# Maxima and turned blocks in one ring of four banks, value products in four blocks, maxima and scores over 64 rows each

## The chip, the core and the metric

The kernel runs on one core of one Trainium2 chip. The metric is the device time of one launch in microseconds. Engines are named as in the profile: PE (TensorE, matmuls; PEld is its weight loads), DVE (VectorE), ACT (ScalarE), POOL (GpSimd) and SP (SyncE, which here only issues DMAs).

## What is computed

The input x is 16 sequences of 512 tokens with 512 features. Four blocks are added to it in turn, each on a layer-normed x: a gated delta rule (the first layer), an FFN with LoRA experts, the attention that the change touches, and the same FFN again. The attention, cut to what matters:

```python
qh = q.reshape(b, s, N_QUERY, N_HEAD, D_HEAD)      # 4 x 8 heads of 16
kh = k.reshape(b, s, N_HEAD, D_HEAD)               # 8 heads of k and v
scores = jnp.einsum('bsqhd,bthd->bqhst', qh, kh) * scale
probs = jax.nn.softmax(scores, axis=-1)
a_dot = jnp.einsum('bqhst,bthd->bsqhd', probs, vh)
...
a_mem = sigma_q @ memory / (sigma_q @ memory_norm)
out = a_dot * (1.0 - w) + a_mem * w
```

## The kernel before

The first layer (up to about 2100 us) is a program of its own, `delta_rule_layer`, and no part of the change. The rest is `token_layers`: for each of 16 batches (b) an `attention(b, following)` and a `between(b, following)`. `between` holds the two FFNs and the projections of the next attention; part of the next batch's first FFN already runs at the end of `attention`. Every engine has its own hand-written order of the same steps, and semaphores join them.

PSUM is one tensor `ps` (`row_psum`) of eight banks of 128 x 512 fp32. In the attention banks 0 to 2 hold scores (STACK_BANKS = 3), banks 3 to 5 maxima (MAX_BANKS = 3), bank 6 the sums over the values, and bank 7 everything that is turned; the memory products use 6 and 7.

A head has 16 features; to keep fp32 accuracy in fp32r matmuls, q and k are stacked in parts: `q_stack` holds per pair of heads 64 rows for the even and 64 for the odd head, and `k_stack` holds for each head of k the same 128 rows with the other head's 64 rows zeroed. One row of the 64 takes the negative maximum, so that the score comes out already shifted.

`attention` runs in rounds g = 0 to 44. Round g does:

- `maximum(g, st)` for the four token tiles st of head g: a matmul 128x512 (L1618) into a bank, from which DVE takes the row maximum (L1900, `smax`). It waits for `max_ready` of the reduce three tiles back.
- `score(h, tt)` for the four tiles of head h = g - 7 (SCORE_LAG): the matmul with q and k swapped (L1631) into a bank 0 to 2; ACT writes exp into `probs` (L1361), which has 7 slots for heads. It waits for `exp_ready` three tiles back.
- in every fourth round the maxima of four heads (a "quad") are turned (L1673, four transposes of `smax`), ACT copies them negated into `shift` (L1368), and four small DMAs on SP write them into `q_stack`, for which the scores of these heads wait (`shift_in`).
- `values(quad, half)`: the probabilities of four heads times `v_aug` (L1642), 128x32 tiles side by side, eight matmuls in each of two blocks per quad, in rounds with (i, j) in AV_SLOTS = ((1, 1), (3, 0)); j is the half of the round. ACT copies the sum (L1377, `av_sb`), PE turns it (L1691), DVE divides by the sums of exp (L1890, L1894, `av_n`), and POOL adds it to x (L1243).
- in rounds 5 to 8 `memory(t)`: matmuls with `mem_aug` (L1605), and DVE's L1875 to L1880.

Each head's exp may overwrite a slot of `probs` when the values of the head seven before are done:

```python
if h >= PROBS and tt == 0:
    act.wait_ge(av_mm, at(b, 2 * QUADS, 2 * ((h - PROBS) // 4 + 1)))
```

The order within half a round on PE is: maximum, score, [transposes of the maxima], [a value block], maximum, score. In the picks of k (L1577, L1578: `pick_k`) the matmuls take 32 rows each, at different rows of the array.

## Time and profile before

| | us |
|---|---|
| median of 3 runs | 5277.39 |
| lowest, highest | 5273.88, 5286.0 |
| the profiled execution's own time | 5281.24 |
| its span, first to last instruction | 5279.4 |
| mean granted TensorE clock | 0.965 |
| PE busy (share of the span) | 4795.7 (91%) |
| DVE busy | 3613.9 (68%) |
| ACT busy | 2392.5 (45%) |

Busy is the union of an engine's instructions. Matmuls are pipelined, so two that start 0.23 us apart are each shown with some 0.4 us, and a PE that is busy all the time may still wait; the spacing of starts tells more. The trace names tiles by their partitions: `probs` in a row can also be the memory's or the norm's scratch, which share its room. The attention of one batch that the rows below come from (batch 4) runs from 2969.9 to 3106.0 us of the span.

### The profile page before, as it was taken

To read this page: it belongs to the slowest core of one execution; us is meant where nothing else is said; L and a number is where in the kernel's file an instruction comes from. 1 tells how busy PE (TensorE), PEld (TensorE's weight loads), DVE (VectorE), ACT (ScalarE), POOL (GpSimd) and SP (SyncE) were. 2 spreads that over 40 slices of the span, in tenths; PEclk is the share of its full clock that TensorE was granted. 3 is DMA by queue.
4 is the path that set the end of the run, shared out by engine and by line. 5 is a ranking of instruction groups with operands and counts; after the bars stand their busy time and mean duration, and the time that the engine had idled before them with its cause. 6 is when DMAs were issued, how large, how long until landed. Compare 5 with 4: busy or idle time off the path is not lost.

```text
span 5279.4 us, 144356 instructions
## 1 busy us (share of the span) xinstructions
PE 4795.7 (91%) x63104; PEld 3487.2 (66%) x63104; DVE 3613.9 (68%) x7890; ACT 2392.5 (45%) x4592; POOL 714.3 (14%) x909
## 2 busy tenths in 40 slices
PE   4799999999999995799999999999999999999998
PEld 4678877777787774565665665665665665666564
DVE  3667776666677673667767767767766766766765
ACT  2234333333333342346446446445545545545544
POOL 0000000000000000121121121121122121121121
PEclk9899999989999997899999999999999999999999
DMA  2223222222222222000000000000000000000000
GB/s 59 52 63 75 60 60 64 64 62 65 70 59 60 67 68 59 27 1 17 17 9 9 17 17 1 17 17 1 17 17 1 17 17 1 17 17 1 17 9 9
DMA packets 352132, 171.74 MB, mean 33 GB/s; under 512 B 300016, under 2 KB 300784, under 8 KB 350736
## 3 DMA queue, kind: packets, MB, share of 16 engines
q1 hardware_dynamic: 342528, 145.20, 10.4%
q10 hardware_dynamic: 8976, 17.30, 1.2%
q8 instruction: 499, 8.18, 0.7%
q14 instruction: 129, 1.06, 0.1%
HBM read 93.74 MB, written 67.63 MB: 31 GB/s over the span
## 4 chain that ended last, share of the span: by engine, by line
PE 45%; DVE 10%; ACT 3%; issue 1%; DMA 1%; POOL 1%; SPq 0%; DVEq 0%; ACTq 0%; POOLq 0%
PE row_psum L1642 9%; PE row_psum L1631 8%; PE row_psum L1618 8%; DVE smax L1900 5%; PE row_psum L40 5%; PE row_psum L42 5%; PE row_psum L41 5%; PE row_psum L1673 1%; ACT xr_hi L1287 1%; PE row_psum L1691 1%; ACT probs L1361 1%; DVE probs L1880 1%; PE row_psum L1426 1%; PE row_psum L1605 1%; PE row_psum L1586 0%
## 5 line engine op out<-in xcount | busy, mean ns | idle before, releaser
L1900 DVE TENSOR_REDUCE smax<-row_psum 128x1 f32<-128x512 f32 x2048 | 1261.9, 683 | 271.0 <-PE row_psum L1618 270.3
L1361 ACT ACTIVATE probs<-row_psum 128x512 f32<-128x512 f32 x2048 | 1080.8, 607 | 592.9 <-PE row_psum L1631 370.6
L1618 PE MATMUL row_psum<-k_stack,q_stack 128*128 128x512 f32 x2048 | 864.8, 431 | 33.3 <-DVE smax L1900 24.4
L1631 PE MATMUL row_psum<-q_stack,k_stack 128*128 128x512 f32 x2048 | 849.0, 426 | 25.1 <-ACT probs L1361 19.6
L1618 PEld LDWEIGHTS row_psum<-k_stack,q_stack 128*128 128x128 f32 x2048 | 389.6, 191 | 359.4 <-DVE smax L1900 231.7
L1631 PEld LDWEIGHTS row_psum<-q_stack,k_stack 128*128 128x128 f32 x2048 | 385.9, 191 | 267.3 <-ACT probs L1361 161.7
L1642 PE MATMUL row_psum<-probs,v_aug 128*32 128x512 f32 x4096 | 489.2, 598 | 0.0
L868 DVE TENSOR_TENSOR lane_t<-lane_t,lane_p 128x30 f32<-128x30 f32 (+14 forms) x960 | 318.4, 332 | 32.9
L865 DVE TENSOR_TENSOR lane_p<-lane_t 128x30 f32<-128x30 f32 (+14 forms) x960 | 316.2, 329 | 23.5
L40 PE MATMUL span_bank<-x_hi,w_hi 128*128 128x256 f32 x1024 | 304.8, 298 | 30.2 <-DVE x_lo L841 30.1
L40 PE MATMUL row_psum<-wf_hi,xr_hi 128*128 128x320 f32 (+1 forms) x1024 | 327.4, 320 | 0.5 <-DVE xr_lo L1768 0.3
L42 PE MATMUL row_psum<-wf_hi,xr_lo 128*128 128x320 f32 (+1 forms) x1024 | 319.8, 312 | 0.0
L41 PE MATMUL row_psum<-wf_lo,xr_hi 128*128 128x320 f32 (+1 forms) x1024 | 318.8, 311 | 0.0
L41 PE MATMUL span_bank<-x_lo,w_hi 128*128 128x256 f32 x1024 | 291.9, 285 | 0.6 <-issue 0.6
L42 PE MATMUL span_bank<-x_hi,w_lo 128*128 128x256 f32 x1024 | 292.0, 285 | 0.0
L1243 POOL TENSOR_TENSOR xs<-xs,av_n 128x256 f32<-128x256 f32 x128 | 93.4, 729 | 1452.3 <-DVE av_n L1894 1452.3
L263 POOL TENSOR_TENSOR o_lo<-og_both,o_hi 128x512 fp32r<-128x512 f32 x64 | 93.1, 1474 | 1328.2 <-DVE tri L883 1242.1
L1642 PEld LDWEIGHTS row_psum<-probs,v_aug 128*32 128x32 f32 x4096 | 108.4, 109 | 220.7 <-issue 185.8
L366 ACT ACTIVATE og_both<-og_both 128x512 f32<-128x512 f32 x64 | 40.3, 630 | 468.1 <-DVE og_both L918 468.1
L40 PEld LDWEIGHTS span_bank<-x_hi,w_hi 128*128 128x128 f32 x1024 | 199.0, 194 | 42.8 <-ACT x_hi L299 34.7
L1890 DVE RECIPROCAL av_rc<-row_psum 128x16 f32<-128x16 f32 x128 | 32.2, 252 | 277.7 <-PE row_psum L1691 277.7
L1327 ACT ACTIVATE q_stack<-row_psum 128x512 fp32r<-128x512 f32 x256 | 154.1, 609 | 148.8 <-PE row_psum L1586 145.3
(209 smaller groups left out, 9816.1 us busy)
## 6 DMA issues: line engine op xcount, KB each, us to landing
x_sp<-in_x ACTq DMA_DIRECT2D x33, 512.0 KB, 4.0
tri_dram<-tri SPq DMA_DIRECT2D x256, 64.0 KB, 2.0
lane_t<-tri_dram SPq DMA_DIRECT2D x32, 512.0 KB, 4.8
inv_dram<-lane_t SPq DMA_DIRECT2D x32, 512.0 KB, 2.6
inv_b<-inv_dram SPq DMA_DIRECT2D x256, 64.0 KB, 2.3
x_res<-in_x SPq DMA_DIRECT2D x32, 512.0 KB, 3.8
x<-x_res SPq DMA_DIRECT2D x32, 512.0 KB, 3.8
xs<-x SPq DMA_DIRECT2D x16, 1024.0 KB, 5.5
```

The lines of the kernel that those rows point to most:

```text
L40: pe.matmul(out, a_hi, b_hi, start=first, stop=False)
L41: pe.matmul(out, a_hi, b_lo, start=False, stop=False)
L42: return pe.matmul(out, a_lo, b_hi, start=False, stop=last)
L865: mark(dve.tensor_tensor(prod, lane_t[:, 0:m, m:m + 1].to_broadcast([P, m, n]), lane_t[:, m:m + 1, m + 1:NB].to_broadcast([P, m, n]), ALU. ...
L868: mark(dve.tensor_tensor(lane_t[:, 0:m, m + 1:NB], lane_t[:, 0:m, m + 1:NB], prod, ALU.add))
L1243: pool.tensor_tensor(xq, xq, av_n[:, :, :, :].rearrange("p t h e -> p t (h e)"), ALU.add).then_inc(adot_added, 1)
L1327: act.activation(q_stack[:, m, :], ps[:, (HP + m) % STACK_BANKS, :], ACT.Copy).then_inc(qstack_ready, 1)
L1361: act.activation(probs[:, h % PROBS, tt, :], ps[:, m % STACK_BANKS, :], ACT.Exp, scale=float(DH) ** -0.5).then_inc(exp_ready, 1)
L1618: pe.matmul(ps[:, STACK_BANKS + m % MAX_BANKS, :], q_stack[:, qt, P * st:P * st + P], k_stack[:, kv, :], start=True, stop=True).then_inc(m ...
L1631: pe.matmul(ps[:, m % STACK_BANKS, :], k_stack[:, kv, P * tt:P * tt + P], q_stack[:, qt, :], start=True, stop=True).then_inc(score_mm, 1)
L1642: last = pe.matmul(ps[32 * e:32 * e + 32, 6, :], v_aug[:, tt, h % NKV, :], probs[:, h % PROBS, tt, :], start=tt == 0, stop=tt == NT - 1)
L1900: dve.tensor_reduce(smax[:, g, st:st + 1], ps[:, STACK_BANKS + (NT * g + st) % MAX_BANKS, :], AX.X, ALU.max).then_inc(max_ready, 1)
```

## The change

Three things change, all in `attention`.

First, the maxima's banks, the transposes of the maxima (maxT) and the turned values (avT) share one ring. `ring_of_banks` walks through the rounds when the program is built and gives each user the bank that was given out longest ago; before round 9 the ring is banks 3, 4, 5, from round 9 bank 7 joins it (it belonged to the memory products until then). The last quad's maxT and the avT from round 31 on keep bank 7. Each user waits for whoever was in its bank before (`ring_bank`), and for nothing else.

Second, `values` has four blocks per quad, one per tile tt, at the start of four rounds in a row (j == 0). The order of accumulation is the same. `exp` waits tile by tile for them where the head is the last of a quad.

Third, while maxima and scores run in the same round (maxima in rounds 7 to 31, scores of heads 0 to 24), their matmuls read only the 64 rows of their own head (`rows_of`): maximum g the rows of kv = g % 8, score g - 7 those of the other half. The rows left out are the zeroed ones of `k_stack`.

```diff
 SCORE_LAG = 7
 AV_LAG = SCORE_LAG + 1
-AV_SLOTS = ((1, 1), (3, 0))
...
-MAX_BANKS = 3
+RING = (3, 4, 5)
+RING_LAST = 7
...
+        def ring_of_banks():
+
+            order, place, inside = list(RING), {}, {RING_LAST: ("memory", NT - 1)}
+
+            def put(kind, n, bank=None):
+                bank = order[0] if bank is None else bank
+                order.remove(bank)
+                order.append(bank)
+                place[kind, n] = bank, inside[bank] if bank in inside else None
+                inside[bank] = kind, n
+
+            for g in range(NH + OUT_LAG):
+                if g == MEM_LAG + NT:
+                    order.insert(0, RING_LAST)
+                for st in range(NT):
+                    if g < NH:
+                        put("max", NT * g + st)
+                    quad, i = divmod(g - MAXT_LAG, 4)
+                    if (i, st) == (0, 2) and 0 <= quad < QUADS:
+                        put("maxT", quad, RING_LAST if quad == QUADS - 1 else None)
+                quad, i = divmod(g - 3 - TURN_LAG, 4)
+                if i == 0 and 0 <= quad < QUADS:
+                    put("avT", quad, RING_LAST if 4 * quad + 3 + TURN_LAG >= NH - 1 else None)
+            return place
...
+                                if h >= PROBS and h % 4 == PROBS % 4 and tt:
+                                    act.wait_ge(av_mm, at(b, NT * QUADS, NT * ((h - PROBS) // 4) + tt + 1))
                                 if h >= PROBS and tt == 0:
-                                    act.wait_ge(av_mm, at(b, 2 * QUADS, 2 * ((h - PROBS) // 4 + 1)))
+                                    act.wait_ge(av_mm, at(b, NT * QUADS, NT * ((h - PROBS) // 4) + (1 if h % 4 == PROBS % 4 else NT)))
...
+            def rows_of(kv, paired):
+
+                return slice(64 * (kv % 2), 64 * (kv % 2) + 64) if paired else slice(0, P)
+
             def attention(b, following):
 
                 def memory(t):
...
-                        pe.wait_ge(shift_ready, at(b, QUADS, 1))
...
+                def ring_bank(kind, n):
+
+                    bank, inside = in_ring[kind, n]
+                    if inside is not None:
+                        of, k = inside
+                        if of == "max":
+                            pe.wait_ge(max_ready, at(b, NT * NH, k + 1))
+                        elif of == "maxT":
+                            pe.wait_ge(shift_ready, at(b, QUADS, k + 1))
+                        elif of == "avT":
+                            pe.wait_ge(avn_ready, at(b, QUADS, k + 1))
+                        else:
+                            pe.wait_ge(amem_ready, at(b, NT, k + 1))
+                    return bank
+
                 def maximum(g, st):
...
-                    elif m >= MAX_BANKS:
-                        pe.wait_ge(max_ready, at(b, NT * NH, m - MAX_BANKS + 1))
-                    pe.matmul(ps[:, STACK_BANKS + m % MAX_BANKS, :], q_stack[:, qt, P * st:P * st + P], k_stack[:, kv, :],
+                    bank = ring_bank("max", m)
+                    rows = rows_of(kv, g >= SCORE_LAG)
+                    pe.matmul(ps[:, bank, :], q_stack[rows, qt, P * st:P * st + P], k_stack[rows, kv, :],
                               start=True, stop=True).then_inc(max_mm, 1)
...
-                    pe.matmul(ps[:, m % STACK_BANKS, :], k_stack[:, kv, P * tt:P * tt + P], q_stack[:, qt, :],
+                    rows = rows_of(kv, h + SCORE_LAG < NH)
+                    pe.matmul(ps[:, m % STACK_BANKS, :], k_stack[rows, kv, P * tt:P * tt + P], q_stack[rows, qt, :],
                               start=True, stop=True).then_inc(score_mm, 1)
 
-                def values(quad, half):
-
-                    pe.wait_ge(exp_ready, at(b, NT * NH, NT * (4 * quad + 3) + 2 * half + 2))
-                    if half == 0 and quad:
+                def values(quad, tt):
+
+                    pe.wait_ge(exp_ready, at(b, NT * NH, NT * (4 * quad + 3) + tt + 1))
+                    if tt == 0 and quad:
                         pe.wait_ge(av_ready, at(b, QUADS, quad))
...
                             pe.wait_ge(max_ready, at(b, NT * NH, 16 * quad + 16))
-                            if quad:
-                                pe.wait_ge(shift_ready, at(b, QUADS, quad))
-                            if quad == 1:
-                                pe.wait_ge(amem_ready, at(b, NT, NT))
-                            if turned_before(quad):
-                                pe.wait_ge(avn_ready, at(b, QUADS, turned_before(quad)))
+                            bank = ring_bank("maxT", quad)
...
                         quad, i = divmod(g - 3 - AV_LAG, 4)
-                        if (i, j) in AV_SLOTS and 0 <= quad < QUADS:
-                            values(quad, AV_SLOTS.index((i, j)))
+                        if j == 0 and 0 <= quad < QUADS:
+                            values(quad, i)
```

The order on PE in a round with transposes of the maxima (round 28), from its first maximum on, before (L1618 maximum, L1631 score, L1673 those transposes, L1642 a value block):

```order
L1618 MATMUL row_psum<-k_stack,q_stack 128x512 [waits max_ready,qstack_ready]
L1631 MATMUL row_psum<-q_stack,k_stack 128x512 [waits exp_ready]
L1618 MATMUL row_psum<-k_stack,q_stack 128x512 [waits max_ready]
L1631 MATMUL row_psum<-q_stack,k_stack 128x512 [waits exp_ready]
L1618 MATMUL row_psum<-k_stack,q_stack 128x512 [waits max_ready]
L1631 MATMUL row_psum<-q_stack,k_stack 128x512 [waits exp_ready]
L1673 MATMUL row_psum<-ident,smax 4x128 [waits avn_ready,shift_ready,max_ready]
L1673 MATMUL row_psum<-ident,smax 4x128 x3
L1642 MATMUL row_psum<-probs,v_aug 32x512 [waits av_ready,exp_ready]
L1642 MATMUL row_psum<-probs,v_aug 32x512 x7
L1618 MATMUL row_psum<-k_stack,q_stack 128x512 [waits max_ready]
L1631 MATMUL row_psum<-q_stack,k_stack 128x512 [waits exp_ready]
```

And in the same round now (L1661 maximum, L1675 score, L1713 transposes, L1687 a value block):

```order
L1661 MATMUL row_psum<-k_stack,q_stack 128x512 [waits max_ready,qstack_ready]
L1675 MATMUL row_psum<-q_stack,k_stack 128x512 [waits exp_ready]
L1687 MATMUL row_psum<-probs,v_aug 32x512 [waits exp_ready]
L1687 MATMUL row_psum<-probs,v_aug 32x512 x3
L1661 MATMUL row_psum<-k_stack,q_stack 128x512 [waits max_ready]
L1675 MATMUL row_psum<-q_stack,k_stack 128x512 [waits exp_ready]
L1661 MATMUL row_psum<-k_stack,q_stack 128x512 [waits max_ready]
L1675 MATMUL row_psum<-q_stack,k_stack 128x512 [waits exp_ready]
L1713 MATMUL row_psum<-ident,smax 4x128 [waits avn_ready,max_ready]
L1713 MATMUL row_psum<-ident,smax 4x128 x3
L1661 MATMUL row_psum<-k_stack,q_stack 128x512 [waits max_ready]
L1675 MATMUL row_psum<-q_stack,k_stack 128x512 [waits exp_ready]
```

The eight value matmuls behind the transposes have become four behind the round's first score (the other four of that eight now come one round earlier, in the same place); the transposes no longer wait for `shift_ready`, and a maximum of the next round does instead.

The order on ACT before, from the first round in which the values are summed (L1361 exp, L1377 the copy av_sb):

```order
L1361 ACTIVATE probs<-row_psum 128x512 [waits score_mm] x4
L1361 ACTIVATE probs<-row_psum 128x512 [waits av_mm,score_mm]
L1361 ACTIVATE probs<-row_psum 128x512 [waits score_mm]
L1377 ACTIVATE av_sb<-row_psum 128x512 [waits av_mm]
L1361 ACTIVATE probs<-row_psum 128x512 [waits score_mm] x2
L1361 ACTIVATE probs<-row_psum 128x512 [waits av_mm,score_mm]
L1361 ACTIVATE probs<-row_psum 128x512 [waits score_mm] x3
L1361 ACTIVATE probs<-row_psum 128x512 [waits av_mm,score_mm]
L1361 ACTIVATE probs<-row_psum 128x512 [waits score_mm] x3
```

And now (L1386 exp, L1402 av_sb):

```order
L1386 ACTIVATE probs<-row_psum 128x512 [waits score_mm] x4
L1386 ACTIVATE probs<-row_psum 128x512 [waits av_mm,score_mm] x2
L1402 ACTIVATE av_sb<-row_psum 128x512 [waits av_mm]
L1386 ACTIVATE probs<-row_psum 128x512 [waits av_mm,score_mm] x3
L1386 ACTIVATE probs<-row_psum 128x512 [waits score_mm] x3
L1386 ACTIVATE probs<-row_psum 128x512 [waits av_mm,score_mm]
```

The instructions stand in the same order; where four exps of the last head of a quad waited once for all of the value products, each now waits for its own tile's.

## Rows read from the trace of the kernel before

**Rows 1.** The page's first line.
```profile
span 5279.4 us, 144356 instructions
```

**Rows 2.** Windows: one batch's stages; start:end, length, busy time of each engine (instructions), clock.
```profile
2969.90:2995.70 25.80, 22.79 (x100) 14.96 (x101) 24.24 (x49) 14.22 (x26) 4.26 (x4) 1.00 0.01 4
2995.70:3008.30 12.60, 10.60 (x43) 7.30 (x41) 11.11 (x22) 8.22 (x16) 2.10 (x2) 0.86 0.01 1
3008.30:3071.20 62.90, 62.83 (x349) 34.04 (x347) 48.68 (x85) 43.19 (x86) 2.90 (x4) 1.00 0.01 2
3071.20:3106.00 34.80, 32.23 (x202) 17.34 (x202) 15.66 (x37) 19.18 (x41) 10.90 (x15) 1.00 0.01 2
3106.00:3164.40 58.40, 54.20 (x324) 47.63 (x322) 40.55 (x97) 17.17 (x41) 16.89 (x24) 1.00 0.11 36
```

**Rows 3.** Waits in 3008.28 to 3071.22: who waited for whom; us, times, longest.
```profile
DVE smax L1900 <- PE row_psum L1618: 14.1, 10, 1.8
...
ACT probs L1361 <- PE row_psum L1642: 7.9, 5, 1.6
```

**Rows 4.** The chain that ended last, 3000 to 3075: start us, us, what.
```profile
3022.22 0.47 PE row_psum L1673 x4
...
3061.49 0.47 PE row_psum L1673 x4
```

**Rows 5.** Timeline of PE, 3021.2 to 3026.6: start us, us, instruction, count.
```profile
3021.59 0.39 PE L1618 MATMUL row_psum<-k_stack,q_stack 128*128 128x512 f32 x1
3021.82 0.40 PE L1631 MATMUL row_psum<-q_stack,k_stack 128*128 128x512 f32 x1
3022.09 0.60 PE L1673 MATMUL row_psum<-ident,smax 128*4 128x128 f32 x4
3022.62 1.92 PE L1642 MATMUL row_psum<-probs,v_aug 128*32 128x512 f32 x16
3024.47 0.50 PE L1618 MATMUL row_psum<-k_stack,q_stack 128*128 128x512 f32 x1
```

**Rows 6.** Timeline of DVE, 3013 to 3030; brackets: idle before, and its releaser.
```profile
3017.04 4.28 DVE L1900 TENSOR_REDUCE smax<-row_psum 128x1 f32<-128x512 f32 x7 [1.45 <-PE row_psum L1618]
3021.24 0.25 DVE L1890 RECIPROCAL av_rc<-row_psum 128x16 f32<-128x16 f32 x1
...
3021.86 1.88 DVE L1900 TENSOR_REDUCE smax<-row_psum 128x1 f32<-128x512 f32 x3
```

**Rows 7.** Timeline of ACT, 3013 to 3030.
```profile
3012.64 0.57 ACT L1368 ACTIVATE shift<-row_psum 4x512 fp32r<-4x512 f32 x1
3013.12 2.00 ACT L1361 ACTIVATE probs<-row_psum 128x512 f32<-128x512 f32 x4
```

**Rows 8.** Timeline of PE, 2962.2 to 2964.0: picks of k between products of q.
```profile
2962.66 0.39 PE L42 MATMUL row_psum<-xr_hi,wq_lo 128*128 128x512 f32 x1
2962.97 0.51 PE L1577 MATMUL row_psum<-xat_hi,sel 32*128 32x512 f32 x3
2963.31 0.40 PE L1578 MATMUL row_psum<-xat_lo,sel 32*128 32x512 f32 x3
2963.64 0.50 PE L40 MATMUL row_psum<-xr_hi,wq_hi 128*128 128x512 f32 x1
```

**Rows 9.** Waits in the tail, 3071.2 to 3106.
```profile
PEld row_psum L1631 <- ACT probs L1361: 6.4, 13, 0.8
ACT probs L1361 <- PE row_psum L1642: 6.1, 2, 3.1
```

**Rows 10.** Windows in the first layer, at a fall of the clock.
```profile
1493.20:1498.10 4.90, 4.90 (x129) 4.76 (x128) 4.90 (x10) 2.89 (x6) 0.00 (x0) 1.00 0.65 102
1498.40:1501.80 3.40, 3.40 (x9) 2.64 (x9) 2.92 (x4) 0.00 (x0) 2.27 (x2) 0.50 0.50 76
```

**Rows 11.** Timeline of PE, 1493 to 1503.
```profile
1493.17 5.04 PE L551 MATMUL span_bank<-kq 32*64 32x128 f32 x128
```

**Rows 12.** Timeline of SP's queue, 3012 to 3017.
```profile
3013.24 2.39 SPq L1199 DMA_DIRECT2D q_stack<-shift  x4
```

More of the change, by code:

```diff
@@ L1150, in head, with bank_of @@
             return divmod(4 * quad + i, NKV)
-        def turned_before(quad):
-            return sum(4 * q + 3 + TURN_LAG < 4 * quad + MAXT_LAG for q in range(QUADS))
-        def maxima_before(quad):
-            return sum(4 * q + MAXT_LAG <= 4 * quad + 3 + TURN_LAG for q in range(QUADS))
+        def ring_of_banks():
[19 more added lines that the diff above has]
+            return place
+        in_ring = ring_of_banks()
+        def bank_of(kind, n):
+            return in_ring[kind, n][0]
         def in_order(begin, attention, between):
@@ L1686, in attention @@
                         pe.wait_ge(av_ready, at(b, QUADS, quad + 1))
[L1687 to L1689 removed]
+                        bank = ring_bank("avT", quad)
                         for t in range(NT):
[L1691 removed]
+                            last = pe.transpose(ps[:, bank, P * t:P * t + P], av_sb[:, P * t:P * t + P], ident2[:, :])
                         last.then_inc(avT_mm, 1)
```

29 lines of the change are left out of this document (13 added, 16 removed).

## The prediction

> **What bounds the kernel now.** I read the span first [rows 1], then cut one batch into stages [rows 2]. Batches repeat every 194.5 us, and 16 of them fill the second layer. The five stages are: rounds 0 to 7 (25.8 us), rounds 8 to 11 (12.6 us), rounds 12 to 31 up to the first reduce of round 31 (62.9 us), the tail with the last scores (34.8 us), and the work between two attentions (58.4 us). The reader is to see that the third stage is the longest, that PE is busy in all of it, and that DVE (48.68 of 62.90) and ACT (43.19) are not. "Busy" for PE includes the flight of pipelined matmuls, so the spacing of starts is what counts below.
>
> The chain through that stage passes the transposes of the maxima at regular places, 3022.22 and 3061.49, three periods of four rounds apart [rows 4]: 13.1 us for four rounds. The sum of PE's work in four rounds comes from the spacing of starts [rows 5]. A maximum or a score starts 0.23 us after its predecessor (3021.59, 3021.82), so 32 of them take 7.5 us. A block of value products (16 instructions in the trace, since each of the 8 matmuls is fp32 and runs as two) holds PE for 1.85 us (3022.62 to 3024.47), two blocks 3.7 us. The two groups of four transposes take about 0.5 us each (3022.09 to 3022.62). Together 12.2 us of 13.1; the other 0.9 us are waits. PE is the bound.
>
> DVE comes next. Seven reduces follow each other in 4.2 us, 0.60 us each, and the normalising of four heads takes 0.62 us (3021.24 to 3021.86) [rows 6]. Four rounds need 16 x 0.60 + 0.62 = 10.2 us. The wait table says where the rest goes: DVE waited 14.1 us in this stage for L1618, in ten waits of up to 1.8 us [rows 3], that is, it ran dry in each 1.85 us block. ACT's four exps take 2.00 us including the last one's 0.57, so 0.48 us apart, and a shift copy costs it 0.48 us (3012.64 to 3013.12) [rows 7]. With av_sb priced like the shift, four rounds need 16 x 0.48 + 2 x 0.48 = 8.6 us. ACT also stood 7.9 us before an exp that must not overwrite probabilities until both value blocks are done [rows 3].
>
> **The change, part by part.**
>
> *64 rows in opposite halves.* Heads g and g-7 have kv of opposite parity, so in rounds 7 to 31 the maximum reads one half of the array's rows and the score the other. Does PE run them side by side? The trace has the same kind of matmul: the three picks of k at L1577 are fp32r, 128 columns wide, 512 long, on different 32-row groups and into different banks, and all three stand in one piece of 0.51 us, with the next three beginning 0.34 us after (2962.97, 2963.31) [rows 8]. Three full-height matmuls would need 0.7 us. So I take them as parallel: a pair costs 0.235 us in place of 0.47, 16 pairs 3.8 us instead of 7.5. The lower bound is this; the upper bound is 0.47 (no overlap).
>
> *Changes of tile shape.* The step from full height to 32-row tiles took 0.31 us instead of 0.23 (2962.66 to 2962.97), and back 0.33 us (2963.31 to 2963.64) [rows 8]: 0.1 us per change. The Trainium skill ("TensorEngine Tiling (Array Packing)", Tiling Modes, Key Properties) says that changing the tiling mode drains the engine, which speaks against a change that multiplies such places; by this trace the drain costs about 0.1 us.
>
> *Four value blocks of 4 matmuls.* The matmuls are the same, so a block holds PE for half of 1.85, 0.93 us, plus a change of shape on each side: 1.13 us, four of them 4.5 us instead of 3.7. With the transposes at 1.2 us (their changes included) PE's sum for four rounds is 3.8 + 4.5 + 1.2 = 9.5 us. That is below DVE's 10.2 us. What queues behind a block is a pause of about 1.4 us for DVE (score, block, next maximum), and four banks hold 2.4 us of reduces, where three banks (1.8 us) did not cover 1.85 us plus a score.
>
> *The ring.* The turns no longer own bank 7: a transpose takes the oldest of four banks. What it waits for is a reduce that the next maximum would have waited for anyway, and a maximum that follows in its bank waits for ACT's shift copy (round 4q+5, third tile), about 2 us after the transposes; it is hidden behind three other banks. Transposes of the maxima waited for the normalising of the last turn, and in round 8 for the last memory reduction; the second wait goes. Until round 9 there are only three banks, so rounds 0 to 7 keep their 25.8 us (DVE is busy 24.24 of them [rows 2]).
>
> *ACT's finer waits.* The exp of every fourth head now waits tile by tile; the 7.9 us of waits shrink, but ACT isn't the bound, so they are worth nothing in this stage by themselves.
>
> *The shift through SP.* Four small DMAs take 2.39 us from the first issue [rows 12]. From the transposes to the first score that needs them lie 2.5 rounds, 6.7 us at the new pace. Transposes 0.5, wait for ACT and copy about 1.8, DMAs 2.4: 4.7 us. Covered by 2 us; if the cover went, each 1 us would cost 8 x 16 = 128 us at most.
>
> **The sum.** DVE becomes the bound. The new period lies between 10.2 us (no waits left) and 10.2 + 0.9 (as much waiting as now); blocks are half as long, so I take two thirds of 0.9: 10.8 us. The third stage has 19 rounds, 4.75 periods: 4.75 x (13.1 - 10.8) = 10.9 us. In rounds 8 to 11 DVE is idle 1.5 us (12.60 less 11.11), mostly at the wait that goes: 1.0 us. In the tail ACT stood 6.1 us for value blocks and PE's loads 6.4 us for ACT [rows 9], but the 34.8 us hold much other PE work and the changes of shape grow by 0.6 us; between 0 and 3 us, I take 1.2. Nothing for the last stage. Per batch 13.1 us, for 16 batches 210 us. The profiled execution took 5281.2 us (span 5279.4), the median is 5277.4: 5281.2 - 210 = 5071, against the median 5067. I forecast **5067 us**. With no waits left (14.1 + 1.5 + 1.2 = 16.8 us, 269 us) it is 5008; with 0.9 us of waits and nothing in the tail, 9.5 + 1.0 = 10.5 us, 5109.
>
> **Rivals.**
>
> *Weights of the same half can't be loaded under its running matmul.* Then each half needs load and stream in turn. The first matmuls after a change show this spacing, 0.34 us (2962.97 to 2963.31) [rows 8], for a pair: 16 x 0.34 = 5.4 us, PE's sum 11.1 us, period 11.7, saving 4.75 x 1.4 + 1.5 = 8.2 us per batch, **5147 us**. For it speaks that the trace never has a long run of such pairs; against it, that at full height the next load runs under the current matmul, which the 0.23 us spacing shows [rows 5]. The Trainium skill ("TensorE: Matmul & The Clock Gate", Part 3, The mechanism) says that a weight load overlaps matmuls in flight only when the row group differs or it goes to the background buffer; by its first half the time would be this one. The 0.23 us at full height speaks for the second half.
>
> *The clock.* PE will be less dense. After five microseconds of nothing but 32-row tiles (L551) the granted clock fell from 1.00 to 0.50, that is from 2.4 to 1.2 GHz, for 3.4 us [rows 10, 11], and in rounds 8 to 11, where PE waited, the mean is 0.86 [rows 2]. If 64-row matmuls count for less than full ones and a quarter of the third stage runs at 1.2 GHz, PE's sum is 1.25 x 9.5 = 11.9, period 12.5, saving 2.9 + 1.5 = 4.4 us, **5207 us**. Against it: pairs fill all 128 rows together, the value blocks are full height, and the sum says PE streams some nine tenths of the period. A fall in rounds 8 to 10 alone costs nothing, since a pair at 1.2 GHz (0.47 us) is still shorter than a reduce.
>
> *Slower: the pairs don't overlap.* They are 128 columns wide and each waits on its own semaphore; if the second is held until the first has left the array, PE's sum is 7.5 + 4.5 + 1.2 = 13.2 us, with 0.6 us of waits 13.8: 0.7 us more per period, 3.3 us per batch, less about 1 us of waits saved in rounds 8 to 11: 2.3 x 16 = 37 us, **5314 us**. It decides from a pair spacing of (13.1 - 0.6 - 5.7) / 16 = 0.43 us on. Against it stands L1577.
>
> **How the numbers follow.** DVE-bound as forecast 0.62 (own range 5008 to 5109); same-half loading 0.14; clock 0.09; no overlap 0.09, of which 0.07 end slower and 0.02 the same; something in between that gives back nearly all 0.06 (0.03 faster, 0.03 same). A measurement of this kernel tells some 0.2%, 10 us, from no change. So faster 0.88, same 0.05, slower 0.07. The range takes in the first two cases: 5008 to 5150.
>
> **What would show it.** Right: the period of four rounds falls from 13.1 to 10.4 to 11.1 us; DVE's idle before the reduce in the third stage falls from 14.1 to under 4 us and the chain there passes through the reduces; score and maximum of a pair start within 0.05 us of each other while pairs follow at 0.24 us when nothing waits; the value blocks stand at 0.9 to 1.0 us; rounds 0 to 7 and the last stage keep 25.8 and 58.4 us. Wrong: a pair spacing of 0.34 or 0.47 us in a run of pairs; a granted clock well under 1.00 in the third stage; score waiting for the shift DMAs; or waits moved to ACT, whose three banks are unchanged: if ACT becomes the partner that runs dry, the waits exceed 0.9 us.

## The result, and the profile after

The changed kernel takes **5091.56 us** (median of 4 runs, 5087.94 to 5102.96) against 5280.30 us of the kernel before in the same session (4 runs): ratio 0.9645, 95% interval 0.9628 to 0.9662. Forecast were 5067 us and 5008 to 5150.

The page's first line, and its groups of the reduce and the exp (busy us, mean ns, idle before). On the page of before DVE stood 271.0 us ahead of its reduces.

```profile
span 5091.6 us, 144724 instructions
...
L1938 DVE TENSOR_REDUCE smax<-row_psum 128x1 f32<-128x512 f32 x2048 | 1269.3, 681 | 90.9 <-PE row_psum L1661 90.4
L1386 ACT ACTIVATE probs<-row_psum 128x512 f32<-128x512 f32 x2048 | 1096.6, 602 | 378.1 <-PE row_psum L1675 358.5
```

The windows of one batch's five stages (batch 4), as in [rows 2]: length, busy time of PE, PEld, DVE, ACT, POOL, granted clock.

```profile
2921.90:2948.00 26.10, 22.49 (x99) 14.34 (x100) 24.39 (x48) 14.16 (x26) 4.21 (x4) 1.00 0.01 3
2948.00:2958.80 10.80, 9.76 (x57) 4.77 (x55) 10.73 (x21) 8.15 (x16) 2.17 (x2) 1.00 0.01 2
2958.80:3011.90 53.10, 51.97 (x344) 21.09 (x340) 49.08 (x85) 43.85 (x86) 2.94 (x4) 1.00 0.01 2
3011.90:3045.80 33.90, 30.71 (x201) 16.34 (x194) 15.76 (x37) 19.70 (x40) 10.63 (x15) 1.00 0.01 2
3045.80:3104.20 58.40, 54.24 (x324) 47.63 (x321) 40.41 (x97) 17.08 (x41) 16.90 (x24) 1.00 0.11 37
```

Set against [rows 2], the third stage fell from 62.9 to 53.1 us and the second from 12.6 to 10.8, where the clock is now 1.00 instead of 0.86. The other three moved by less than a microsecond here. DVE is busy 49.08 of 53.10 us in the third stage; it was 48.68 of 62.90. PE still reads 51.97, because a matmul in flight counts as busy; that number doesn't tell whether PE is the bound. The last stage keeps its 58.40.

The waits of that stage, 2958.8 to 3011.9 (compare [rows 3]):

```profile
PEld row_psum L1661 <- DVE smax L1938: 15.9, 19, 0.8
ACT probs L1386 <- PE row_psum L1675: 8.1, 14, 0.8
DVE smax L1938 <- PE row_psum L1661: 3.9, 14, 0.8
PEld row_psum L1675 <- DMA q_stack<-shift: 3.1, 5, 1.1
```

DVE's wait for the maxima fell from 14.1 to 3.9 us, and no wait for value products is among the large ones. What rose is PE's: its weight loads wait 15.9 us for a reduce, where they waited 8.9 before. In [rows 3] DVE mostly waited for PE, now PE waits for DVE. That wait alone proves little, since run e1 below, which PE bounds, has 12.6 us of it; what speaks for DVE as the pace is that it is busy in 92% of the stage (49.08 of 53.10). One sign that the prediction named did not come: the chain of work that ended last doesn't pass through the reduces. In the two traces they are 3.2% of it around this stage now and were 5.1% before; the rest is mostly PE, whose matmuls in flight leave the chain hardly a gap through which to step to another engine.

PE's timeline from 2970.4 (compare [rows 5]; start, us, instruction):

```profile
2970.43 0.39 PE L1661 MATMUL row_psum<-k_stack,q_stack 64*128 64x512 f32 x1
2970.43 0.39 PE L1675 MATMUL row_psum<-q_stack,k_stack 64*128 64x512 f32 x1
...
2971.94 1.06 PE L1687 MATMUL row_psum<-probs,v_aug 128*32 128x512 f32 x8
2972.93 0.49 PE L1661 MATMUL row_psum<-k_stack,q_stack 64*128 64x512 f32 x1
...
2973.27 0.39 PE L1661 MATMUL row_psum<-k_stack,q_stack 64*128 64x512 f32 x1
...
2973.51 0.39 PE L1661 MATMUL row_psum<-k_stack,q_stack 64*128 64x512 f32 x1
```

Maximum and score of a pair start in the same 10 ns, pairs follow at 0.23 to 0.24 us, and a value block of 8 instructions holds PE from 2971.94 to 2972.93, 0.99 us. The first pair after it needs 0.34 us (2972.93 to 2973.27), so the change of shape costs the expected 0.1 us there.

DVE's timeline over one period (compare [rows 6]; in brackets idle time and its releaser):

```profile
2969.52 0.25 DVE L1928 RECIPROCAL av_rc<-row_psum 128x16 f32<-128x16 f32 x1
...
2970.14 3.07 DVE L1938 TENSOR_REDUCE smax<-row_psum 128x1 f32<-128x512 f32 x5
2973.47 2.48 DVE L1938 TENSOR_REDUCE smax<-row_psum 128x1 f32<-128x512 f32 x4 [0.26 <-PE row_psum L1661]
2976.10 2.48 DVE L1938 TENSOR_REDUCE smax<-row_psum 128x1 f32<-128x512 f32 x4 [0.15 <-PE row_psum L1661]
2978.89 1.89 DVE L1938 TENSOR_REDUCE smax<-row_psum 128x1 f32<-128x512 f32 x3 [0.31 <-PE row_psum L1661]
2980.70 0.25 DVE L1928 RECIPROCAL av_rc<-row_psum 128x16 f32<-128x16 f32 x1
```

From reciprocal to reciprocal lie 11.18 us, where 13.1 lay before. Three pauses remain, 0.26 + 0.15 + 0.31 = 0.72 us, each behind a value block.

### The profile page after: what moved, and what is told of

Its sections match the earlier page's. It is cut to its first block, busy times and chain, and to the rows that moved or that the text cites. A ratio compares the mean times of both kernels' runs of the same rounds, so it can differ in the third digit from the quotient of the medians.

```text
span 5091.6 us, 144724 instructions
## 1 busy us (share of the span) xinstructions
PE 4591.6 (90%) x63104; PEld 3229.5 (63%) x63104; DVE 3620.3 (71%) x7890; ACT 2409.6 (47%) x4592; POOL 716.3 (14%) x909
## 3 DMA queue, kind: packets, MB, share of 16 engines
q1 hardware_dynamic: 342528, 145.20, 10.7%
## 4 chain that ended last, share of the span: by engine, by line
PE 43%; DVE 10%; ACT 3%; issue 1%; POOL 1%; DMA 1%; SPq 0%; DVEq 0%; ACTq 0%; POOLq 0%
PE row_psum L1687 9%; PE row_psum L1661 9%; PE row_psum L40 5%; DVE smax L1938 5%; PE row_psum L42 5%; PE row_psum L41 5%; PE row_psum L1675 4%; PE row_psum L1729 1%; ACT xr_hi L1310 1%; PE row_psum L1713 1%; DVE probs L1918 1%; PE row_psum L1451 1%; DVE stats L1772 1%; POOL rstd L1253 1%; PE row_psum L1633 1%
## 5 line engine op out<-in xcount | busy, mean ns | idle before, releaser
L1386 ACT ACTIVATE probs<-row_psum 128x512 f32<-128x512 f32 x2048 | 1096.6, 602 | 378.1 <-PE row_psum L1675 358.5
L1661 PE MATMUL row_psum<-k_stack,q_stack 64*128 64x512 f32 (+1 forms) x2048 | 738.3, 437 | 50.6 <-DVE smax L1938 24.4
L1675 PE MATMUL row_psum<-q_stack,k_stack 64*128 64x512 f32 (+1 forms) x2048 | 761.6, 447 | 17.4 <-DMA q_stack<-shift 4.4
L1661 PEld LDWEIGHTS row_psum<-k_stack,q_stack 64*128 64x128 f32 (+1 forms) x2048 | 350.5, 186 | 504.1 <-DVE smax L1938 374.0
L1687 PE MATMUL row_psum<-probs,v_aug 128*32 128x512 f32 x4096 | 539.5, 604 | 2.3 <-ACT av_sb L1402 0.8
L1675 PEld LDWEIGHTS row_psum<-q_stack,k_stack 64*128 64x128 f32 (+1 forms) x2048 | 340.9, 185 | 211.7 <-ACT probs L1386 152.3
L1315 ACT ACTIVATE probs<-row_psum 128x64 f32<-128x64 f32 x256 | 52.3, 229 | 331.4 <-PE row_psum L42 331.4
```

Source lines behind the costliest of these rows:

```text
L1386: act.activation(probs[:, h % PROBS, tt, :], ps[:, m % STACK_BANKS, :], ACT.Exp, scale=float(DH) ** -0.5).then_inc(exp_ready, 1)
L1661: pe.matmul(ps[:, bank, :], q_stack[rows, qt, P * st:P * st + P], k_stack[rows, kv, :], start=True, stop=True).then_inc(max_mm, 1)
L1675: pe.matmul(ps[:, m % STACK_BANKS, :], k_stack[rows, kv, P * tt:P * tt + P], q_stack[rows, qt, :], start=True, stop=True).then_inc(score_m ...
L1687: last = pe.matmul(ps[32 * e:32 * e + 32, 6, :], v_aug[:, tt, h % NKV, :], probs[:, h % PROBS, tt, :], start=tt == 0, stop=tt == NT - 1)
```

## The experiments

Stages below are medians over the 16 batches, in us, worked out from each trace: rounds 0 to 7, rounds 8 to 11, rounds 12 to 31, the tail (the cuts of [rows 2]; the time between attentions is 58.4 in all of them). "rows" is 64 rows each, "ring" the ring of four banks, "blocks" the four value blocks. The kernel before took 5278.5, 5276.7 and 5283.9 us beside the three groups of experiments (e1 to e4, e5 to e8, e9 to e12); each ratio is taken within its group. Every kernel but the one before and e2 also lets each exp wait for its own tile's values only; no run has that alone.

| | rows, ring, blocks | median us | ratio, 95% | 0-7 | 8-11 | 12-31 | tail |
|---|---|---|---|---|---|---|---|
| before | none | 5277.4 | 1 | 25.85 | 12.70 | 62.96 | 34.62 |
| after | all | 5091.6 | 0.9645 (0.9628-0.9662) | 26.16 | 10.79 | 52.70 | 34.24 |
| e2 | rows | 5282.4 | 1.0002 (0.9982-1.0021) | 25.85 | 12.38 | 63.22 | 34.49 |
| e12 | ring | 5283.1 | 0.9999 (0.9985-1.0014) | 27.12 | 10.80 | 63.43 | 34.85 |
| e9 | blocks | 5255.2 | 0.9958 (0.9941-0.9976) | 25.83 | 12.97 | 61.93 | 33.31 |
| e3 | rows, ring | 5283.9 | 1.0006 (0.9993-1.0019) | 27.17 | 10.79 | 62.53 | 35.66 |
| e1 | ring, blocks | 5235.5 | 0.9916 (0.9887-0.9946) | 26.16 | 10.79 | 61.79 | 34.21 |
| e6 | rows, blocks | 5139.2 | 0.9734 (0.9718-0.9750) | 25.83 | 14.33 | 53.88 | 33.07 |
| e4 | all, same half | 5226.0 | 0.9899 (0.9871-0.9927) | 26.16 | 10.98 | 60.81 | 34.16 |
| e5 | e3, first block half a round earlier | 5257.6 | 0.9965 (0.9949-0.9982) | 26.16 | 10.79 | 61.12 | 36.58 |
| e7 | all, two shift DMAs | 5092.6 | 0.9644 (0.9627-0.9661) | 26.17 | 10.79 | 52.69 | 34.25 |
| e8 | all, block ahead of the score | 5237.6 | 0.9928 (0.9912-0.9943) | 26.15 | 10.79 | 59.61 | 36.38 |
| e10 | e3, half exps | 5204.9 | 0.9853 (0.9834-0.9872) | 27.11 | 10.79 | 59.46 | 35.36 |
| e11 | all, half exps | 5042.2 | 0.9539 (0.9523-0.9556) | 26.16 | 10.79 | 50.65 | 33.34 |

Medians over the batches hide the clock. In rounds 0 to 7 a batch has one of two lengths, in every kernel: where the mean granted clock of the stage was 0.94 or 0.95 instead of 1.00, it took 0.7 to 1.0 us longer. That befell 1 of 16 batches of the kernel before, 3 of the changed kernel, 1 of e1, 6 of e7, but 9 of e3, 10 of e10 and 11 of e12, and so the medians of these three read 27.1 to 27.2. In rounds 12 to 31 the clock stayed at 1.00 in the kernels without long blocks (e8 and e6 dip in one batch) and in those with long blocks and full rows (before, e12); with long blocks and 64 rows (e2, e3, e5, e10) its mean is 0.98. The batches of these four in which it stayed at 1.00 took 61.7, 61.4, 59.5 and 58.2 us.

**e1, all rows again.**

```diff
 def rows_of(kv, paired):
-    return slice(64 * (kv % 2), 64 * (kv % 2) + 64) if paired else slice(0, P)
+    return slice(0, P)
```

> The changed kernel with the ring and the four value blocks, but every maximum and score over all 128 rows. Theory (PE was the bound, and the halves running side by side relieve it): PE's sum for four rounds is 7.5 + 4.0 to 4.5 + 1.2 = 12.7 to 13.2 us, so the period stays at 12.9 to 13.8 us and the time is 5240 to 5320 us; maxima and scores start 0.23 us apart. Rival (the gain comes from the buffering: a fourth bank and shorter blocks keep DVE fed, and PE had slack): the period is 11 to 12 us and the time under 5190 us.

5235.5 us. The third stage is back at 61.8 us. Its window (length, PE, PEld, DVE, ACT, POOL, clock):

```profile
3011.20:3073.00 61.80, 61.80 (x344) 32.89 (x340) 50.05 (x86) 44.43 (x86) 2.92 (x4) 1.00 0.01 1
```

PE is busy in all 61.80 us, and this time the starts say the same: one whole period, from the value block at 3030.47 to that at 3043.53, is 13.06 us, and nothing in it waits: maxima and scores start 0.23 us apart, with 0.1 us more at each change of shape. PE's sum for this case, from the prediction's terms, is 7.5 + 4.5 + 1.2 = 13.2. With full rows and four blocks PE is the bound. By the same starts a block costs 1.00 us and 0.1 on either side. Two blocks of 1.85 us in place of four of 1.00 would make PE's sum an estimated 12.4 us, which is less than the 13.1 of the kernel before.

**e2, the rows alone**: `rows_of` in the kernel before, used by both matmuls as in the change.

> The kernel before with nothing changed but the 64 rows (three banks for the maxima, turns in bank 7, two value blocks of 8 matmuls). Theory: PE's sum falls to about 9.2 us, but a block still keeps PE away for 2.1 us or more while three banks hold 1.8 us of reduces; DVE runs dry by 0.8 to 1.0 us at each of two blocks and the period is 12.0 to 12.4 us, the time 5180 to 5220 us: about half of the gain. Rival (buffering does nothing): the time is that of the changed kernel, 5085 to 5105 us. Second rival (the 64 rows do nothing): 5270 to 5290 us.

5282.4 us, no change, and none of the three forecasts for the right reason: the time is that of the second rival, but the pairs do run side by side, and PE's sum falls by 3.7 us a period, yet the stage keeps its length. The waits of 3009.4 to 3072.7 show where it went (L1623 maximum, L1637 score, L1648 values, L1906 reduce):

```profile
DVE smax L1906 <- PE row_psum L1623: 14.5, 10, 3.2
ACT probs L1361 <- PE row_psum L1637: 12.5, 9, 3.5
ACT probs L1361 <- PE row_psum L1648: 7.9, 5, 1.6
```

DVE waits as long as in [rows 3], ten times, once per block of 1.85 us, and ACT waits 12.5 + 7.9 = 20.4 us. PE has time to spare now, but at places where nobody can use it. A part of the loss is the clock: in the five batches where it stayed at 1.00 the stage took 61.7 us, 1.3 less than before, and in the others, at 0.95 to 0.98, mostly 63.2 or more. In rounds 8 to 11 it fell to 0.60 to 0.86 in every batch. The next runs ask what holds the period at 13 us here.

**e3, the change with two blocks per quad.**

```diff
+AV_SLOTS = ((1, 1), (3, 0))
-    pe.wait_ge(exp_ready, at(b, NT * NH, NT * (4 * quad + 3) + tt + 1))
+    pe.wait_ge(exp_ready, at(b, NT * NH, NT * (4 * quad + 3) + 2 * half + 2))
-    for e in range(4):
+    for tt in (2 * half, 2 * half + 1):
+        for e in range(4):
...
-    if j == 0 and 0 <= quad < QUADS:
-        values(quad, i)
+    if (i, j) in AV_SLOTS and 0 <= quad < QUADS:
+        values(quad, AV_SLOTS.index((i, j)))
```

> The changed kernel (ring, 64 rows) with the values in two blocks of 8 matmuls at their old places. Theory: four banks hold 2.4 us, PE is away 2.0 + 0.3 + 0.3 us, so DVE runs dry by 0.2 to 0.4 us at two places in place of 0.15 to 0.35 us at four, and four changes of tile shape less: within 15 us of the changed kernel, 5080 to 5110 us. Rival (the spreading is what keeps DVE fed): 1 us more per period, 5150 us or more.

5283.9 us, the rival's side and far above the forecast: with blocks of eight, rows and ring together are worth nothing. DVE's timeline across the two blocks:

```profile
3019.25 1.88 DVE L1940 TENSOR_REDUCE smax<-row_psum 128x1 f32<-128x512 f32 x3
3022.39 3.68 DVE L1940 TENSOR_REDUCE smax<-row_psum 128x1 f32<-128x512 f32 x6 [1.26 <-PE row_psum L1662]
3027.30 4.28 DVE L1940 TENSOR_REDUCE smax<-row_psum 128x1 f32<-128x512 f32 x7 [1.23 <-PE row_psum L1662]
```

and PE's in the same stretch (L1662 maximum, L1715 transposes, L1689 values):

```profile
3019.48 0.60 PE L1715 MATMUL row_psum<-ident,smax 128*4 128x128 f32 x4 [0.21 <-DVE av_n L1934]
3020.01 1.92 PE L1689 MATMUL row_psum<-probs,v_aug 128*32 128x512 f32 x16
3021.86 0.49 PE L1662 MATMUL row_psum<-k_stack,q_stack 64*128 64x512 f32 x1
...
3023.54 0.50 PE L1662 MATMUL row_psum<-k_stack,q_stack 64*128 64x512 f32 x1 [0.72 <-ACT shift L1394]
```

DVE is dry for 1.26 and 1.23 us. The transposes wait for DVE's `av_n` (3019.48), and PE has given DVE only three maxima since; then 0.53 us of transposes, 1.85 us of block and the start of a new maximum stand against 1.88 us of reduces. The fourth bank of the ring holds the transposes here, not a maximum. After three more maxima the next one needs that bank and waits 0.72 us for ACT's shift copy, which itself is late, since ACT was dry for 2.20 us behind the same block.

**e4, both in the same half**: the maxima of rounds 7 to 31 read the half of the score.

```diff
-    rows = rows_of(kv, g >= SCORE_LAG)
+    rows = rows_of(kv + 1 if g >= SCORE_LAG else kv, g >= SCORE_LAG)
```

> The changed kernel with the maximum of rounds 7 to 31 reading the rows of the other head of its pair, so that maximum and score lie in the same half of the array (the maxima of these rounds are then not the right ones; the work is the same in size). Theory (it is the opposite halves that let two matmuls run at once, and weights load under a running matmul in the same half too): starts are 0.23 us apart, PE's sum is 12.7 to 13.2 us, the time 5240 to 5320 us, as over 128 rows. Rival (weights of the same half cannot be loaded under its running matmul): starts are 0.34 us apart, PE's sum 16 to 17 us, the time over 5500 us. Second rival (64 rows are faster by themselves): 5090 us.

5226.0 us, close to e1 (5235.5). PE's timeline (L1661 maximum, L1675 score):

```profile
2991.97 0.39 PE L1661 MATMUL row_psum<-k_stack,q_stack 64*128 64x512 f32 x1
2992.20 0.39 PE L1675 MATMUL row_psum<-q_stack,k_stack 64*128 64x512 f32 x1
2992.43 0.38 PE L1661 MATMUL row_psum<-k_stack,q_stack 64*128 64x512 f32 x1
```

Starts of one half lie 0.23 us apart, as at full height: they don't overlap, and the loads cost nothing. (Per batch 20 starts of this stage still lie within 20 ns of another, against 66 in the changed kernel, probably where the half changes from one round to the next; that would explain the 1.0 us by which e4's stage is shorter than e1's, and was not followed up.) So the gain of the rows is that they are opposite halves, not that they are fewer, and the 0.34 us spacing of [rows 8] is a cost of the change of shape, not of loading the same half. The Trainium skill ("TensorE: Matmul & The Clock Gate", Part 3, What overlaps and what doesn't) says that a weight load overlaps running matmuls only when the row group differs. This run does not agree: matmuls of one row group follow each other at 0.23 us with a load between each two.

**e5, e3 with the first block before the transposes.**

```diff
-AV_SLOTS = ((1, 1), (3, 0))
+AV_SLOTS = ((1, 0), (3, 0))
```

> As the run with two value blocks (ring, 64 rows), but the first block stands behind the round's first score instead of behind the transposes of the maxima. Theory (the block behind the transposes delayed the score, the exp and so ACT's shift copy, for which a maximum in the ring waits: 9.4 us per batch of such waits): the waits of the maximum for the shift go, the period falls from 13.0 to 11.6 to 12.1 us, the time is 5140 to 5190 us. Rival (a block of 1.85 us is simply too long for the buffers, wherever it stands): 5260 to 5290 us.

5257.6 us, the rival's side; the third stage fell by 1.4 us only, and by 1.9 in the batches at full clock (61.4 to 59.5). DVE's waits fell from 13.4 to 12.3 us, and its waits are still ten of up to 2.2 us: with the transposes out of the block's way most of the loss stays. It takes the short blocks, not another place for the long one.

**e6, no ring**: four blocks and rows, with the banks and waits of before.

```diff
-                bank = order[0] if bank is None else bank
-                order.remove(bank)
-                order.append(bank)
+                bank = RING[n % 3] if kind == "max" else RING_LAST
...
+                        pe.wait_ge(shift_ready, at(b, QUADS, 1))
```

> The changed kernel (64 rows, four value blocks) without the ring: maxima in banks 3 to 5 in turn, both kinds of transposes in bank 7 with their old waits. Theory (short blocks and the relieved PE give most, the fourth bank covers the rest): DVE holds 1.8 us while PE is away 1.0 + 0.1 + 0.3 us, so it hardly runs dry; the maxima's transposes wait for the normalising again; period 11.4 to 12.0 us, time 5100 to 5160 us. Rival (the fourth bank is decisive): period 12.5 us or more, over 5200 us.

5139.2 us, 47.6 more than with the ring. In the third stage the ring is worth only 1.2 us per batch (53.88 less 52.70), and the tail takes the same back (33.07 against 34.24). Its worth lies in rounds 8 to 11, 3.5 us per batch. Windows there, and PE's timeline (L1712 transposes, L1686 values):

```profile
2959.60:2962.70 3.10, 1.16 (x9) 0.71 (x7) 2.97 (x8) 0.60 (x1) 0.85 (x1) 1.00 0.00 0
2962.80:2966.00 3.20, 3.20 (x13) 1.60 (x13) 1.54 (x3) 1.51 (x4) 1.18 (x1) 0.52 0.00 0
...
2969.80:2971.60 1.80, 1.80 (x9) 0.20 (x8) 0.72 (x2) 0.60 (x1) 0.00 (x0) 0.50 0.00 0
```

```profile
2962.78 0.91 PE L1712 MATMUL row_psum<-ident,smax 128*4 128x128 f32 x4 [2.03 <-DVE probs L1917]
...
2969.81 1.93 PE L1686 MATMUL row_psum<-probs,v_aug 128*32 128x512 f32 x8
2971.68 0.79 PE L1660 MATMUL row_psum<-k_stack,q_stack 64*128 64x512 f32 x1
```

The transposes wait 2.03 us for the last memory product to be read out (L1917). In 2959.6 to 2962.7 PE was busy 1.16 of 3.10 us; then the granted clock is 0.52 and 0.50, that is 1.2 GHz (for 10.2 us in all, 2962.92 to 2973.16), and the value block lasts from 2969.81 to 2971.68, 1.87 us instead of 0.99. Behind it DVE was dry for 1.98 us. With the ring that wait is gone and the clock stays at 1.00 (second window of the changed kernel above).

**e7, the shift rows in two DMAs**: each writes the two rows of one parity.

```diff
-    for i in range(4):
-        n, h = head(quad, i)
-        r0 = 64 * (h % 2) + 3 * DH
-        sp.dma_start(q_stack[r0:r0 + 1, n * HP + h // 2, :], shift[i:i + 1, :]).then_inc(shift_in, 16)
+    for e in range(2):
+        r0 = 64 * e + 3 * DH
+        sp.dma_start(q_stack[r0:r0 + 1, c0:c0 + 2, :], shift[e:4:2, :]).then_inc(shift_in, 16)
```

> The changed kernel with the shift written to q_stack in two DMAs of two rows each instead of four of one row. Each issue takes about 0.6 us of the queue, so the last lands 1.2 us earlier. Theory (the scores of each fourth round wait 0.4 to 1.1 us for the DMA, and DVE runs dry by 0.3 to 0.8 us behind that): the waits for the DMA go, 0.15 to 0.45 us less per period, 5060 to 5085 us. Rival (this wait is covered by the banks, DVE being the bound): unchanged, 5085 to 5105 us.

5092.6 us, no change, because there was little to gain. The wait table above charges five idle stretches of the scores' weight loads to the DMAs, 3.1 us. But in four of the five the last DMA had landed 0.4 us before the load began, and e7 has the same stretches with nothing to release them (the changed kernel, then e7):

```profile
2976.85 0.18 PEld L1675 LDWEIGHTS row_psum<-q_stack,k_stack 64*128 64x128 f32 x1 [0.52 <-DMA q_stack<-shift]
...
2976.76 0.18 PEld L1676 LDWEIGHTS row_psum<-q_stack,k_stack 64*128 64x128 f32 x1 [0.52 <-issue]
```

Only once in this stage did PE itself stand still for a DMA, 0.63 us before the scores of round 27, and there the chain of the changed kernel passes through it:

```profile
2994.72 0.58 ACT shift L1393
2995.31 0.50 SPq L1222
...
2997.12 2.61 DMA q_stack<-shift
...
2999.77 0.50 PE row_psum L1675
```

The issues on SP take 0.5 to 0.6 us each, and this last DMA lands 2.61 us after its issue begins; the usual time is 1.7 us, and 17 of the 128 last DMAs of the changed kernel took 2.1 to 3.6. In rounds 12 to 31 of all 16 batches PE stood still ten times at such a score, for 0.15 to 0.87 us; in e7 it never did. The median stage is as long (52.69 against 52.70), the mean 0.15 us shorter, some 2 us in 16 batches, which this measurement can't tell from nothing.

**e8, the block ahead of the round's first score.** The call of `values` moved from behind `score(h, 0)` to before it.

> The changed kernel with the value block ahead of the round's first score instead of behind it. Theory (a score that waits for ACT holds up the block and the maxima behind it; the block itself waits for an older exp only): DVE's gaps of 0.15 to 0.36 us behind the blocks shrink, 0.2 to 0.6 us less per period, 5050 to 5080 us. Rival (ACT then gets its scores later and runs dry, and the rows of this pair no longer run side by side, 0.23 us more of PE per round): 5095 to 5150 us.

5237.6 us, outside both forecasts: one position costs 146 us. Waits of 2988 to 3048:

```profile
PEld row_psum L1675 <- ACT probs L1386: 18.4, 25, 0.8
ACT probs L1386 <- PE row_psum L1675: 17.4, 20, 1.5
DVE smax L1938 <- PE row_psum L1661: 8.9, 18, 0.8
```

ACT and PE wait for each other, 17.4 and 18.4 us. ACT has only three banks, 1.43 us of exps, and with the score behind the block it goes dry for up to 1.5 us. The chosen place, behind the first pair, hides a block of 1 us for both engines at once. The block also splits a pair here, so that its two matmuls no longer run together; that is at most 0.23 us a round, 0.9 of the 1.45 us by which the period grew. The run doesn't tell the two apart.

**e9, the blocks alone**: e6 with `rows_of` as in e1.

> The kernel before with the values in four blocks alone (no ring, all 128 rows). Theory (PE's sum is one limit, the buffers against the blocks' length the other, and only together do they go): PE is still the bound with 12.7 to 13.0 us for four rounds and four more changes of tile shape, so the time is 5250 to 5300 us. Rival (shorter blocks give 35 us or more by themselves, whatever the rows): under 5245 us.

5255.2 us, 22 us less by the ratio, mostly from the third stage and the tail (1.0 and 1.3 us per batch). PE is busy 62.00 of 62.00 us of its stage, as in e1, and the stage is as long. With full rows four short blocks stop at PE's sum of 13.0 us, which their own changes of shape have raised from 12.4.

**e12, the ring alone**: e3 with `rows_of` as in e1.

> The kernel before with the ring of banks alone (two value blocks, all 128 rows). Theory: PE's sum of 12.2 us and ACT's three banks stay, only the second transposes' wait in round 8 goes (1.5 us per batch) and the wait of the maxima for the shift comes: 5255 to 5290 us. Rival (the fourth bank feeds DVE through the block, and that is worth something without the rest): under 5250 us.

5283.1 us, no change. Rounds 8 to 11 fall to 10.8 us as in every kernel with the ring, and rounds 0 to 7 and the third stage give the 1.9 us back (+1.3 and +0.5). Of the 1.3 only 0.3 are the ring's own; the rest is the lowered clock in 11 of its batches. Kernels whose rounds 0 to 7 are the same (the changed one, e1, e7) have that in 3, 1 and 6, so it can't be put down to the ring alone.

**e10, e3 with half exps, and e11, the changed kernel with half exps.**

```diff
-    act.activation(probs[:, h % PROBS, tt, :], ps[:, m % STACK_BANKS, :], ACT.Exp,
+    act.activation(probs[:, h % PROBS, tt, 0:SEQ // 2], ps[:, m % STACK_BANKS, 0:SEQ // 2], ACT.Exp,
```

Half of the exps are left out, and one memset of the probabilities ahead of the second layer is added (9.9 us on POOL in e11's trace).

> As the run with ring, 64 rows and two value blocks, but each exp of the scores takes 256 of the 512 columns (half of the probabilities is left out; a memset of the tile at the start of the second layer adds up to 12 us once). To be read by the stage of rounds 12 to 31, 62.5 us with whole exps. Theory (with long blocks it is ACT that sets the pace: its three banks hold 1.4 us of exps against a block of 1.85 us, so it runs dry twice per period and its 8.6 us become 12.9): an exp takes some 0.27 us, ACT's sum falls to 5.3 us, the stage to 51 to 56 us. Rival (the maxima's four banks don't cover the block either, DVE sets the pace): 59 us or more.

> The changed kernel with each exp of the scores over 256 of the 512 columns (half of the probabilities is left out; the same memset). To be read by the stage of rounds 12 to 31, 52.7 us with whole exps, DVE's own sum being about 48. Theory (what is left above DVE's sum is scores that wait for ACT and hold up blocks and maxima behind them): 49 to 50.5 us. Rival (what is left is the block against the maxima's banks): 52 to 53 us.

e10 took 5204.9 us, its third stage 59.5; e11 5042.2, its third stage 50.65. An ACT of little more than half the work (29.4 of 58.9 us busy) gets three of the missing ten microseconds in e10, so ACT's speed is a smaller part of what long blocks cost. DVE's timeline of e10 shows which pause went:

```profile
2994.53 3.68 DVE L1941 TENSOR_REDUCE smax<-row_psum 128x1 f32<-128x512 f32 x6 [1.27 <-PE row_psum L1663]
2998.80 4.27 DVE L1941 TENSOR_REDUCE smax<-row_psum 128x1 f32<-128x512 f32 x7 [0.59 <-PE row_psum L1663]
```

The pause at the block behind the transposes is the same 1.27 us; that at the second block fell from 1.23 to 0.59, probably since scores no longer held up the maxima between the two blocks, and more of them stood ready. In e11 the period is 50.65 / 4.75 = 10.7 us: of the 0.9 us by which the changed kernel exceeds DVE's 10.2, ACT has 0.4. DVE is then busy 48.82 of 50.60 us. That is the best sign that DVE sets the pace; no run changes DVE's own work.

No version with the whole computation was faster than the changed kernel; e7 equals it.

## Why the prediction held, point by point

**What bounds the kernel.** "PE is the bound" was the step that had the mechanism wrong. The prediction's own sum gave PE 12.2 us of a period of 13.1, and the rest was not a consequence of it. Two limits lie close together. One is PE's sum with full rows: 12.4 us with two blocks, 13.0 with four (e1 and e9). The other is blocks of 1.85 us against three banks of reduces and of exps: e2 and e3, with PE's sum reduced, still need 13.3 and 13.2 us, and 13.0 and 12.9 in their batches at full clock. The kernel before was held by the second. Removing one limit gave 0 us (e2) or 22 us (e9), removing both 138 us (e6), and with the ring 189. The prediction saw both numbers (DVE "ran dry in each 1.85 us block") but counted the gaps as waits beside PE's sum and took two thirds of them as staying. That its time came out right is in part luck: the change lifts both limits, so a wrong answer to which of them holds cost nothing.

**64 rows in opposite halves.** 0.235 us a pair: 0.23 to 0.24 measured, and e4 shows that it takes opposite halves. The same-half rival (5147 us) described a cost that does not exist; e4 followed at 0.23 us. The rival without overlap also fell, but e1 and e4 show its price: without overlap the kernel is at 5226 to 5236, not at the 5314 forecast. That rival added 0.6 us of waits to a sum of 13.2; e1 needs 13.0 in all.

**The clock.** This rival did not come: the granted clock was 1.00 in the third stage of all 16 batches. It comes, to a small part, where long blocks meet 64 rows (0.98 in e2 and e3).

**Blocks.** 0.93 us plus 0.2: measured 0.99, and 0.1 on either side (e1).

**New period.** Forecast 10.8 us; here 11.18. The sum of 10.2 us left out that each group of reduces costs more than 0.60 us a piece, since a single one lasts 0.68 us and only those in a row start every 0.60: groups of 5, 4, 4 and 3 take 3.07, 2.48, 2.48 and 1.89 us, some 0.08 us each over it. That is 0.3 us, and the pauses are 0.72 where 0.6 were taken. The third stage saved 10.3 us instead of 10.9 by the medians.

**The ring.** Rounds 8 to 11 saved 1.9 us, not 1.0, since the wait for the memory products was also paid in the clock. Windows of the kernel before, with that wait and behind it:

```profile
2996.80:3000.20 3.40, 1.40 (x9) 1.14 (x9) 2.32 (x7) 0.84 (x2) 1.27 (x1) 1.00 0.00 0
3000.30:3003.70 3.40, 3.40 (x10) 2.62 (x9) 2.99 (x6) 2.88 (x6) 0.00 (x0) 0.50 0.02 2
```

The wait of 2.0 us stands in all 16 batches before, the fall in 12. The four without it took 11.8 us, so the wait itself is the forecast 1.0 and the clock the other 0.9. "A fall in rounds 8 to 10 alone costs nothing" was wrong, as e6 shows: the block is what gets too long. In the rest the ring is worth about nothing net. Rounds 0 to 7 are 0.3 us longer, against "keep their 25.8 us". In round 4 the first transposes now wait for one of the three banks: they start 0.48 us behind the maximum (2933.88 to 2934.36), where they followed at 0.23 (2981.85 to 2982.08) when bank 7 was theirs.

**ACT's finer waits and the tail.** Forecast 1.2 us in the tail, measured 0.4; this term was too large. Its waits after the change (compare [rows 9]):

```profile
ACT probs L1386 <- PE row_psum L1675: 9.6, 11, 1.7
PEld row_psum L1675 <- ACT probs L1386: 6.7, 9, 0.8
```

The 6.1 us for value products are gone, but ACT's wait for scores, 5.0 us before, is 9.6, and PE's for ACT 6.7 instead of 6.4. Without the ring the tail gained 1.6 us (e6), so part of it is lost to the turns' new order; which, is open.

**The shift through SP.** "Covered by 2 us" was wrong by a term: the 2.39 us of [rows 12] are four issues, not the landing of the last. In the changed kernel the transposes start at 2970.75, the copy ends at 2972.9, the last DMA lands at 2976.43, 3.5 us after the first issue, and the first score that needs the rows starts at 2976.88. So 0.4 us of cover are left. That is nearly always enough, and by e7 the rest costs some 2 us in all.

**Waits moved to ACT.** To a part, and within the range: with half the exps the third stage is 2.05 us per batch shorter and the kernel 49 us.

**The sum.** By medians 16 x (10.3 + 1.9 + 0.4 - 0.3) = 197 us; by means over the batches, which count those with a lower clock, 16 x (10.1 + 1.7 + 0.5 - 0.4) = 190. Measured are 189, forecast were 210. The miss of 21 us is nearly all in the period (0.8 us a batch), the tail (0.7) and rounds 0 to 7 (0.4), less the 0.7 that rounds 8 to 11 gave more. The other 3 to 4 us between 5067 and 5092 are mostly the kernel before, whose median is 5280.3 us beside the changed kernel and was 5277.4 in the forecast. Terms missed on both sides, so the time is a little nearer than its terms.

## What to carry to other kernels

When the busiest engine's sum and the period nearly agree, ask a second question before believing in one bound: how long is the longest uninterrupted piece on that engine, and how many microseconds of work do the banks of its consumers hold? If both come near the period, an edit against either shows little or nothing alone, and "no effect" is no verdict on it. Cut the long pieces first, place them where all consumers have just been fed (e8), and look for waits of some 2 us on PE: here they were paid again in the clock in most batches. And before a listed wait is attacked, see whether what it waited for had long arrived (e7).

## What the runs showed of the hardware

- Two fp32r matmuls of 64 x 128, 512 long, in opposite halves start in the same 10 ns; in one half they follow at 0.23 us like full ones, each with its own weight load (e4).
- A stretch in which PE was busy 1.16 of 3.10 us (e6) was followed by 10.2 us at 1.2 GHz. In the kernel before, the same wait of 2.0 us was followed by 3.4 us at 1.2 GHz in batch 4 (3000.28 to 3003.69), and the clock fell in 12 of its 16 batches. The pause of 0.63 us in the third stage of the changed kernel (ahead of 2999.77) left the clock at 1.00; in e3, with pauses of 0.72 us, the stage's mean is 0.98.
- Four DMAs of one row each, issued in a row on SP, take 0.5 to 0.6 us apiece, and the last usually lands 1.7 us after its issue began (2.1 to 3.6 in 17 of 128).
